# A two-layer attention and expert kernel in float32: three rounded passes for part of the down products

## The reference, cut to what matters

```python
# first layer: 8 experts of 512 hidden units, the best 2 by router
h = gelu(einsum('td,edh->eth', xf, W1) + b1, approximate=False)
out = einsum('etd,te->td', einsum('eth,ehd->etd', h, W2) + b2, weights)
# second layer: 32 experts of 64 hidden units, the best 6, and a shared one
o = silu(xf @ gate.T) * (xf @ up.T) @ dn.T      # each expert, times its weight c
out = routed + silu(xf @ shared_gate.T) * (xf @ shared_up.T) @ shared_down.T
```

## Time and profile before

| what | value |
|---|---|
| median of 3 runs | 594.29 us |
| the profiled execution's own time | 594.72 us |
| its span | 592.9 us |
| TensorE busy | 566.6 us, 96% |
| VectorE busy | 399.4 us, 67% |
| ScalarE busy | 323.7 us, 55% |
| GpSimd busy | 104.6 us, 18% |
| mean granted TensorE clock | 0.994 |

### The profile page before, as it was taken

The page is one execution under the profiler, slowest core; times in us unless marked ns, Lnnn a source line. Parts: engine busy times, 40 slices in busy tenths (PEclk is TensorE's granted clock), DMA queues, the critical chain, the costliest instruction groups (busy, mean ns, idle before and its releaser), DMA issues.

```text
span 592.9 us, 8098 instructions
## 1 busy us (share of the span) xinstructions
PE 566.6 (96%) x2512; PEld 372.9 (63%) x2512; DVE 399.4 (67%) x1265; ACT 323.7 (55%) x566; POOL 104.6 (18%) x120
## 2 busy tenths in 40 slices
PE   2799999999999999999999999999899999999997
PEld 2666667665666666656676567565667766676664
DVE  4889899783212444648557675778889899677564
ACT  1478687867445466844775458854385342343221
POOL 3102020000211210242122315235200011100000
PEclk9899999999999999999999999999899999999999
DMA  2601000030211120111101021053211332342441
GB/s 78 233 19 28 1 10 2 2 143 19 58 49 36 38 71 19 35 38 36 36 35 36 2 64 36 20 175 112 89 72 53 112 109 87 113 141 67 134 138 40
DMA packets 23306, 38.35 MB, mean 65 GB/s; under 512 B 3776, under 2 KB 9536, under 8 KB 22880
## 3 DMA queue, kind: packets, MB, share of 16 engines
q1 hardware_dynamic: 22832, 37.44, 19.9%
q10 hardware_dynamic: 432, 0.40, 0.3%
HBM read 36.45 MB, written 1.38 MB: 64 GB/s over the span
## 4 chain that ended last, share of the span: by engine, by line
PE 84%; DVE 7%; ACT 4%; issue 3%; DMA 1%; POOL 1%; ACTq 0%; DVEq 0%
PE ps L1682 17%; PE ps L1493 10%; PE ps L1495 9%; PE ps L1494 9%; PE ps L1852 9%; PE ps L1569 4%; PE ps L1488 4%; PE ps L1589 3%; PE ps L1500 2%; PE ps L1604 2%; PE ps L1601 2%; PE ps L1759 2%; PE ps L1739 1%; PE ps L1749 1%; DVE NM L1156 1%
## 5 line engine op out<-in xcount | busy, mean ns | idle before, releaser
L1493 PE MATMUL ps<-xThi,w1s 128*128 128x512 f32 x256 | 144.4, 564 | 2.1 <-DVE h L1445 2.1
L911 ACT ACTIVATE h<-ps,early 128x512 f32<-128x512 f32 x128 | 86.8, 687 | 79.5 <-PE ps L1495 65.7
L1682 PE MATMUL ps<-h,w2s 128*128 128x512 f32 x256 | 122.1, 594 | 0.2 <-DVE ty L1245 0.2
L1495 PE MATMUL ps<-xTlo,w1s 128*128 128x512 f32 x256 | 101.4, 396 | 0.0
L1494 PE MATMUL ps<-xThi,w1s 128*128 128x512 f32 x256 | 100.8, 394 | 0.0
L1002 ACT ACTIVATE s<-ps 128x512 f32<-128x512 f32 x68 | 40.7, 599 | 101.2 <-PE ps L1495 100.9
L1493 PEld LDWEIGHTS ps<-xThi,w1s 128*128 128x128 f32 x256 | 48.6, 190 | 36.5 <-issue 16.9
L1682 PEld LDWEIGHTS ps<-h,w2s 128*128 128x128 f32 x256 | 46.7, 189 | 33.4 <-issue 24.1
L1445 DVE TENSOR_TENSOR h<-s,ps 128x512 f32<-128x512 f32 x68 | 46.5, 684 | 28.7 <-PE ps L1495 25.8
L1494 PEld LDWEIGHTS ps<-xThi,w1s 128*128 128x128 f32 x256 | 48.8, 190 | 25.9 <-issue 21.4
L1852 PE MATMUL ps<-h,w2s 128*128 128x512 f32 x128 | 64.2, 594 | 0.9 <-DVE h L1451 0.9
(11 more groups left out here) (264 smaller groups left out, 884.8 us busy)
## 6 DMA issues: line engine op xcount, KB each, us to landing
CB<-ct_rows SPq DMA_DIRECT2D x128, 128.0 KB, 2.9
WB<-wt_rows SPq DMA_DIRECT2D x32, 256.0 KB, 3.2
w2s<-w_dram SPq DMA_DIRECT2D x2, 2048.0 KB, 8.1
raw<-gu_dram SPq DMA_DIRECT2D x4, 512.0 KB, 5.5
x_in<-x_dram SPq DMA_DIRECT2D x4, 256.0 KB, 2.8
w2s<-dn_dram SPq DMA_DIRECT2D x1, 1024.0 KB, 7.2
out_dram<-ty SPq DMA_DIRECT2D x4, 256.0 KB, 2.9
late<-late_dram SPq DMA_DIRECT2D x1, 608.5 KB, 7.5
```

The lines of the kernel that those rows point to most:

```text
L911: nc.scalar.activation(h32[:, c % HR, :], bank[c % 2], ACT.Gelu, bias=b1T[:, c:c + 1]).then_inc(b_gelu.sem, 1)
L1493: M(dst, w[0], xThi[:, x, :], start=start, stop=False)
L1495: return M(dst, w[0], xTlo[:, x, :], start=False, stop=stop)
L1682: M(bank[2], w2s[:, c * P:(c + 1) * P], h32[:, c % HR, :], start=(c % 4 == 0), stop=(c % 4 == 3)).then_inc(b_y.sem, 1)
```

## The change

- **First layer, odd chunks.** `second` does a full float32 matmul for even c as before. For odd c it calls `down3`: three float32r passes with high and low halves of the weights and of h. ScalarE rounds h to the high half (`highs_b`, into hh0), VectorE subtracts it from h32 in place (`lows_b`).
- **Second layer, batches 2 and 3** (`THREE` = 2). `downs` calls `down3` for all 17 chunks. ScalarE rounds (`highs_d`, into hh1), GpSimd subtracts in place (`lows_d`).
- **Weights.** The odd blocks of w2 are split once, in two steps (`split2`): ScalarE rounds to w2h, GpSimd writes the rest over the odd blocks. Those of the second layer are split in one small and four further steps (`split3`).
- **Space.** hh0 lies over s32 and hh1 over WB; `twins` gives a tensor a second name of type float32r. So the first silus of stage D wait for the last down product of stage B, and the first roundings of `highs_d` for the last ty.
- **Order.** All five tables are written anew. Among the changes: the pieces of `split0` come earlier on ScalarE and VectorE; `split2`, `split3`, `highs_b`, `highs_d`, `lows_b` and `lows_d` are merged in. A down product of stage D, batch 2 or 3, stands behind the gate and up products of the third chunk after its own.

The diff, without the tables:

```diff
+    def twins(name, shape):
+        with nc.sbuf_tensor(name, shape, F32) as plain:
+            pass
+        return plain, sb(name + "_r", shape, F32R)
...
-    h32 = sb("h32", [P, 4, S])
+    h32, h32r = twins("h32", [P, 4, S])
...
-    w2s = sb("w2s", [P, NC0 * P])
+    w2s, w2r = twins("w2s", [P, NC0 * P])
...
+    w2h = sb("w2h", [P, NP1 * P], F32R)
+    odd, odd_low = (w.rearrange("p (c two k) -> p c two k", two=2, k=P)[:, :, 1, :] for w in (w2s[:], w2r[:]))
+    gus, dns, dn_low = w1s, w2s[:, 0:NP1 * P], w2r[:, NP1 * P:]
...
+    shh = sb("shh", [P, 2, P], F32R)
...
+    WB, hh1 = twins("WB", [P, 2, S])
+    s32, hh0 = twins("s32", [P, 2, S])
...
+        def split2():
+            for k in range(2):
+                yield
+                pool.wait_ge(w2_hi.sem, w2_hi.at(0, k + 1))
+                o, c = slice(8 * k, 8 * k + 8), slice(1024 * k, 1024 * k + 1024)
+                nc.gpsimd.tensor_tensor(odd_low[:, o, :], odd[:, o, :], w2h[:, c].bitcast(F32).rearrange("p (c k) -> p c k", k=P),
+                                        ALU.subtract).then_inc(w2_lo.sem, 1)
...
+        def lows_d(b):
+            for n in range(ND):
+                yield
+                t = b * ND + n
+                pool.wait_ge(d_hi.sem, d_hi.at(b - THREE, n + 1))
+                nc.gpsimd.tensor_tensor(h32r[:, t % HR, :], h32[:, t % HR, :], hh1[:, t % 2, :].bitcast(F32), ALU.subtract).then_inc(d_lo.sem, 1)
...
+        def split3():
+            for k in range(NDN):
+                yield
+                w, hi, _ = down1_piece(k)
+                act.wait_ge(down1_loaded.sem, 32)
+                if k:
+                    act.wait_ge(b_y.sem, b_y.at(NB - 1, NC0))
+                copy(hi, w).then_inc(dn_hi.sem, 1)
+
+        def highs_b(b):
+            for j in range(NC0 // 2):
+                yield
+                act.wait_ge(b_gelu.sem, b_gelu.at(b, 2 * j + 2))
+                if b or j >= 2:
+                    act.wait_ge(b_y.sem, b_y.at(b, 2 * j - 2))
+                copy(hh0[:, j % 2, :], h32[:, (2 * j + 1) % HR, :]).then_inc(b_hi.sem, 1)
+
+        def highs_d(b):
+            for n in range(ND):
+                yield
+                t = b * ND + n
+                if n:
+                    act.wait_ge(d_h.sem, d_h.at(b, n))
+                else:
+                    act.wait_ge(d_t.sem, d_t.at(b, 1))
+                if b == THREE and n < 2:
+                    act.wait_ge(b_ty.sem, b_ty.at(NB - 1, E0))
+                if b > THREE or n >= 2:
+                    act.wait_ge(d_dn.sem, d_dn.at(b, n - 1))
+                copy(hh1[:, t % 2, :], h32[:, t % HR, :]).then_inc(d_hi.sem, 1)
...
                 if b * ND + n >= 2:
                     act.wait_ge(d_t.sem, d_t.at(b, n - 1))
+                else:
+                    act.wait_ge(b_y.sem, b_y.at(NB, 0))
                 nc.scalar.activation(s32[:, (b * ND + n) % 2, :], bank[0], ACT.Silu).then_inc(d_silu.sem, 1)
...
+        def lows_b(b):
+            for j in range(NC0 // 2):
+                yield
+                dve.wait_ge(b_hi.sem, b_hi.at(b, j + 1))
+                o = (2 * j + 1) % HR
+                V.tensor_tensor(h32r[:, o, :], h32[:, o, :], hh0[:, j % 2, :].bitcast(F32), ALU.subtract).then_inc(b_lo.sem, 1)
...
+        def down3(dst, w, x, start, stop):
+            (whi, wlo), (xhi, xlo) = w, x
+            M(dst, whi, xhi, start=start, stop=False)
+            M(dst, wlo, xhi, start=False, stop=False)
+            return M(dst, whi, xlo, start=False, stop=stop)
...
-                pe.wait_ge(b_gelu.sem, b_gelu.at(b, c + 1))
-                M(bank[2], w2s[:, c * P:(c + 1) * P], h32[:, c % HR, :], start=(c % 4 == 0), stop=(c % 4 == 3)).then_inc(b_y.sem, 1)
+                j, at, ends = c // 2, c % 4 == 0, c % 4 == 3
+                if c % 2:
+                    pe.wait_ge(b_lo.sem, b_lo.at(b, j + 1))
+                    if b == 0 and j % 8 == 0:
+                        pe.wait_ge(w2_lo.sem, w2_lo.at(0, j // 8 + 1))
+                    w = w2h[:, j * P:(j + 1) * P], odd_low[:, j, :]
+                    down3(bank[2], w, (hh0[:, j % 2, :], h32r[:, c % HR, :]), at, ends).then_inc(b_y.sem, 1)
+                else:
+                    pe.wait_ge(b_gelu.sem, b_gelu.at(b, c + 1))
+                    M(bank[2], w2s[:, c * P:(c + 1) * P], h32[:, c % HR, :], start=at, stop=ends).then_inc(b_y.sem, 1)
...
+                    if b == THREE and (n == 0 or n % 4 == 1):
+                        pe.wait_ge(dn_lo.sem, dn_lo.at(0, 1 + (n + 3) // 4))
+                    pe.wait_ge(d_lo.sem, d_lo.at(b - THREE, n + 1))
+                    w = (w2h[:, c], dn_low[:, c]) if n else (shh[:, 0, :], shh[:, 1, :])
+                    down3(bank[2], w, (hh1[:, t % 2, :], h32r[:, t % HR, :]), n == 0, n == ND - 1).then_inc(d_dn.sem, 1)
```

More of the change, by code:

```diff
@@ L98, in at, with followed @@
         return self.first + b * self.per + k
+    def followed(self, b, per):
+        return Signal(self.sem, per, self.at(b, 0))
     def then(self):
@@ new lines @@
+    "group": [[2308, 2422, 2471, 2536, 2585, 2658, 3106], [2885, 3005, 3057, 3198, 3250, 3312, 3563], [3612, 3726,
[6 rows of a table added]
+    "output": [[5367], [8235], [11171], [13967]],
+    "prepare_b": [[11471, 13093, 13421], [15774, 17441, 19113], [22548, 22842, 24890], [27761, 29459, 32131]],
+    "base": [[15341], [20854], [26847], [33153]],
+    "gelus": [[13724, 13910, 14066, 14122, 14343, 14484, 14683, 14776, 14934, 15071, 15282, 15419, 15577, 15714, 15916,
[11 rows of a table added]
+    "highs_b": [[14016, 14193, 14631, 14994, 15142, 15637, 15826, 16214, 16509, 16948, 17185, 17392, 17866, 18170,
[4 rows of a table added]
@@ new lines @@
+    "output": [[5551], [8475], [11367], [14183]],
+    "norm_b": [[6977, 7353, 7907, 8597, 8717, 9059, 9982, 10033], [11111, 12924, 13097, 13248, 13267, 13302, 14302,
+        14353], [15764, 15854, 16134, 17515, 17629, 19465, 20866, 21076], [21975, 22113, 22286, 22305, 23291, 24599,
+        27273, 27626]],
+    "halves_b": [[12178, 13103], [17071, 17124], [24294, 24526], [29186, 30166]],
+    "routing": [[12006, 12835, 12875, 12884, 13166, 13188, 13209, 13230], [16005, 16027, 17105, 17115, 17598, 17619,
+        18531, 18598], [22759, 22780, 22821, 23173, 23195, 23281, 24094, 24185], [29133, 29155, 29221, 29506, 30855,
+        31023, 31045, 31341]],
@@ L284 @@
-    "output": [[5284, 5469], [8255, 8400], [11078, 11321], [13928, 14122]],
-    "prepare_b": [[11246, 11941, 13215], [14616, 17403, 19227], [21950, 23460, 24985], [28049, 28674, 32812]],
-    "first": [[13373, 13698, 13973, 14050, 14211, 14280, 14745, 14814, 15200, 15354, 15423, 15667, 15736, 15976, 16045,
[8 rows of a table removed]
-    "weights": [[13839], [20434], [26532], [34737]],
-    "second": [[14355, 14441, 14527, 14659, 14886, 15028, 15114, 15268, 15495, 15581, 15804, 15890, 16117, 16203,
[8 rows of a table removed]
-    "stage_c": [[14984, 16873, 19672, 20123, 20256, 20342], [26690, 27144, 27328, 28559], [33727, 33890, 34160, 34246]
-        , [40154, 41299, 41483, 42633]],
@@ new lines @@
+    "output": [[5216, 5442], [8169, 8365], [11076, 11258], [13880, 14073]],
+    "prepare_b": [[10980, 11896, 13301], [15697, 15896, 18976], [21589, 22649, 24214], [27697, 28208, 32011]],
+    "first": [[13175, 13649, 13925, 14001, 14163, 14395, 14464, 14687, 14756, 14914, 15107, 15330, 15399, 15557, 15827,
[8 rows of a table added]
+    "weights": [[13791], [19652], [26540], [33047]],
+    "second": [[14237, 14326, 14533, 14619, 14828, 14983, 15176, 15262, 15471, 15626, 15741, 15985, 16195, 16349,
[8 rows of a table added]
+    "stage_c": [[15063, 17751, 19264, 19876, 20060, 20146], [26211, 26494, 26629, 26784], [32700, 33000, 33205, 33497]
+        , [39251, 39922, 40281, 40599]],
@@ L911, in gelus, with split2, split3 @@
                 nc.scalar.activation(h32[:, c % HR, :], bank[c % 2], ACT.Gelu, bias=b1T[:, c:c + 1]).then_inc(b_gelu.sem, 1)
+        def split2():
+            for k in range(2):
+                yield
+                act.wait_ge(down0_loaded.sem, 16)
+                c = slice(1024 * k, 1024 * k + 1024)
+                copy(w2h[:, c].rearrange("p (c k) -> p c k", k=P), odd[:, 8 * k:8 * k + 8, :]).then_inc(w2_hi.sem, 1)
+        def split3():
+            for k in range(NDN):
+                yield
[13 more added lines that the diff above has]
+            for n in range(ND):
+                yield
+                t = b * ND + n
[8 more added lines that the diff above has]
+                copy(hh1[:, t % 2, :], h32[:, t % HR, :]).then_inc(d_hi.sem, 1)
         def stage_c(b):
@@ L1470, in _ @@
                ("feed", map(feed, every)), ("norm_d", map(norm_d, every)),
-               ("halves_d", map(halves_d, every)), ("router", map(router, every)), ("stage_d", map(stage_d, every)))
+               ("halves_d", map(halves_d, every)),
+               ("lows_b", map(lows_b, every)), ("router", map(router, every)), ("stage_d", map(stage_d, every)))
     @block.tensor
```

268 lines of the change are left out of this document (140 added, 128 removed), and 188 rows, old and new, of tables (PLAN_ACT, PLAN_DVE, PLAN_PE, PLAN_SP).

## The result

The changed kernel takes **601.29 us** (median of 4 runs, 600.07 to 602.38) against 594.51 for the kernel before beside it: ratio 1.0114, 95% interval 1.0096 to 1.0132. The profiled execution has a span of 599.1 us.

A forecast was written before the change was run, and what follows sets the result against it. It took TensorE's products to bound the kernel. Terms -17.2 + 2.3 + 0.5 + 4.0 + 2.0 + 1.5 = -6.9 us gave 587.8, or 587.4 against the median; range 578.5 to 595.

The forecast's parts named there:

- Products, -17.2: Both layers: 98 down products as three rounded passes, 0.69 instead of 0.866 us, save 0.176 each, 17.2 us in all.
- First layer, "+1.5": First layer: GpSimd's accumulates make 64 VectorE subtractions wait 6.6 us; TensorE sees 1.5 of it (0 to 6.6).
- TensorE hides both, at nothing.: 139 to 405 us: VectorE rises to 183 of 266 us and ScalarE to about 205, costing TensorE nothing.
- Splits of dn, at nothing.: Second layer's down weights: splitting them once on ScalarE and GpSimd adds nothing to the sum.
- Third batch, +4.0: Second layer's third batch: VectorE, also doing the fourth's norm and router, collides with GpSimd's low halves; +4.0 us (0 to 9).
- Fourth batch, +2.3 tail and +2.0: Second layer's last batch: copy and GpSimd step before the last product, +2.3 us; sharing at fill and end, +2.0 (0 to 6).
- First silu's wait, +0.5,: Second layer's start: first silu waits for all 128 first-layer down products, because space is shared; +0.5 us (0 to 2.4).
- Orders, 0: All five queues re-sorted: the w2 load has some 8 us left, and nothing is added.
- The slower one: Last two batches: GpSimd wins each near tie, 2.62 us per chunk instead of 2.246; 599.7 us, chance 0.08.
- The third rival: First layer short of ScalarE: a third of the 64 late by 0.25 us, 5 us; 592.4 us, chance 0.15.
- The clean gain: GpSimd and VectorE fall into step, each using the other's pause, without sharing cost; 579.9 us, chance 0.20.
- the door: VectorE instructions with two SBUF inputs and GpSimd ones reading SBUF exclude each other; sharing terms +4.0, +2.0 and +1.5 us.

The follow-up runs named there:

- e5: Changed kernel without the low half of h: gelu and VectorE's product write h rounded, so no roundings or subtractions of h; 579.15 us, ratio 0.9730.
- e7: Three passes in the first layer only, in the new orders, with VectorE's 64 subtractions left out and ScalarE's copies kept; 585.33 us, ratio 0.9850.
- e8: Changed kernel with GpSimd's 34 second-layer low halves cut to 8 of 512 columns; 592.18 us, ratio 0.9956.
- e14: New orders, three passes only for every fourth first-layer chunk and the second layer's last batch, whose low halves are on VectorE; 593.91 us, ratio 1.0006.
- e18: Changed kernel with the 32 accumulates and the second layer's low halves moved from GpSimd to VectorE; 590.49 us, ratio 0.9948.
- e3: Changed kernel with three passes in the second layer's last two batches only, the first layer's down products in full precision; 600.81 us, ratio 1.0090.
- e6: Changed kernel with the second layer's 34 low halves moved from GpSimd to VectorE; 597.71 us, ratio 1.0056.
- e9: New orders with the old work, plus one unread GpSimd subtraction per chunk in the last two batches; 595.08 us, ratio 1.0017.
- e16: Three passes in the first layer only, in the new orders, with the 32 accumulates moved from GpSimd to VectorE; 588.34 us, ratio 0.9912.
- e19: As e16, with the w1 split's last GpSimd subtraction moved behind the second layer's first norm; 586.13 us, ratio 0.9857.
- e11: Three passes in the first layer only, in the new orders, with VectorE's 64 subtractions cut to 8 of 512 columns; 588.24 us, ratio 0.9910.
- e17: New orders with the old full-precision work, and the 32 accumulates moved from GpSimd to VectorE; 590.99 us, ratio 0.9955.

## Why the prediction was wrong

By its own steps:

- **Products, -17.2.** Right in the unit: 0.175 us measured in the fourth batch (e5), 0.176 said. The passes alone bring 14.7 net, the splits' cost and some stops and clock in stretch B among it.
- **First layer, "+1.5" (0 to 6.6).** This is the step that failed: the subtractions cost 10 us (e7; stretch B 317.2 against 307.2 with the passes alone), 8.5 more than said. It counted how long the subtractions themselves would be held, 6.6 us, and that was near: 64 x (772 - 682) = 5.8 us. Then it let TensorE see a quarter of that, and took the rest of VectorE's work out of the sum. But VectorE works in order: each norm or router step that GpSimd holds (1.25 us for 4 elements per partition) delays the subtraction queued behind it, and the down product's place behind its `first` product is short, in PLAN_PE 2.6 chunks on average for an odd one and 2 or fewer for 30 of the 64, with a chunk of some 1.5 us and gelu, copy and subtraction of 2 us to fit in. The 32 accumulates had stood in the same place before and cost 1.9 us; beside a VectorE that TensorE waits for every second chunk they cost 11.
- **"TensorE hides both, at nothing."** True of ScalarE's copies to within 2 us (e7: 307.6 against 307.2 us). Of VectorE not: 183 of 266 us busy was foretold and 185 came, but an average of 70% does not say that each subtraction is in time. Much of the idle 80 us that I read as cover was spent standing in order: 26 us before the subtractions, for ScalarE's copy.
- **Splits of dn, at nothing.** 1.1 us in the second batch (50.3 to 51.4, in e5, e8, e14, e18 and after), 2.0 in e3 and 1.9 in e6 (52.3 and 52.2); why more there was not looked into.
- **Third batch, +4.0 (0 to 9).** The mechanism was right, the size wrong: 49.8 against 42.1 with passes alone, 7.7, within its bounds. e8 puts 7.0 on GpSimd's step, e9 shows 1.9 of it without any reader. The rest is hold and chain together, and was not split further.
- **Fourth batch, +2.3 tail and +2.0.** 3.0 in all (30.7 against 27.7). The tail is there: the last three down products start 0.26, 1.23 and 0.43 us later than the pace of 0.23 us per pass, 1.9 in all, for 2.3 said. In steady state the hold costs next to nothing (2.11 us per chunk for 2.07) though it comes in almost every chunk, as the prediction had it (0.60 and 1.29 us fit in 2.07).
- **First silu's wait, +0.5,** was not tried alone; batch 0 shows nothing of its size. **Orders, 0:** 0.2% in favour, with a 3.2 us stop of their own; in e16, where it is 3.27, e19's parting leaves 1.16.
- **Rivals.** The slower one gave 599.7, near the result, by a mechanism that isn't it: it asked for 2.62 us per chunk in the last two batches once the two collide every time. In the fourth they collide in almost every chunk, and the chunks stay near 2.1 us; and it kept 9.8 us of gain in the first layer, where none came. The third rival (ScalarE short in the first layer) had the place and the wrong engine. The clean gain came nowhere with the change whole. Of the prediction's own signs, the mean of the product with CB (0.92 and 1.12 us in the last two batches) and the third batch slower than the fourth came true; TensorE idle under 4 us from 139 to 405 did not (9.0). The 0.08 for a slower case was too little above all because the one cost that I knew to be open in both stages, the door, was given a range per batch and none as one common error; that is my reading, no run tests it.

Not settled: how the first layer's 10 us divide between subtractions held themselves and small steps held ahead of them in the queue, which the rows show in single places and no run parts; how the 0.6% that the 8-column subtractions cost (e11) divides between standing behind the copy and the waits of the bank behind it; and why e17 gains 0.2%, more than a control should.

## What to carry to other kernels

Before giving VectorE a step on which TensorE waits, list what GpSimd does in the same stretch: 32 long GpSimd steps that read SBUF cost 1.9 us in all while VectorE had nothing urgent, and 11 us once it had. Price such a hold by what is queued behind the held instruction, tiny steps included, and against the number of chunks by which the order lets the product trail, not by the engine's mean busy share. In the kernel with the first layer's half of the change, moving 32 sums from the idle GpSimd to the busier VectorE, and parting two GpSimd steps, turned a loss of 0.2% into a gain of 1.4%. Then run the control: with its sums moved too, the kernel in full precision gains 0.45%, and only 0.43% of e16's gain is the three-pass products'.
